# Idle TensorE products in front of each pair's inner-layer products and around each pair's sums in a graph-network kernel

## The chip, the cores and the metric

The kernel runs on one core of a Trainium2 chip. The metric is the device time of one execution, in microseconds. The kernel before takes 3646.17 us (median of 3 runs, 3644.92 to 3647.67 us).

## The reference: what is computed

Two graph layers over 6250 nodes of 128 channels and 200000 edges, sorted by target node:

```
h = relu(layernorm(x))
ef  = relu(edge_attr @ We1 + be1) @ We2 + be2          # 64 -> 128 -> 128 per edge
ef  = ef * sigmoid(edge_weight @ Wt + bt)
msg = relu(concat(h[src], ef) @ Wn1 + bn1) @ Wn2 + bn2
x = x + segment_sum(msg, dst) + h                      # first layer
h = relu(layernorm(x))
h = h + segment_sum(h[src], dst)                       # second layer
x = x + relu(relu(h @ W1 + b1) @ W2 + b2)
```

## The kernel before, in words

The edges are cut into 196 pairs of two blocks of 512 edges; four pairs make a body, so the first layer has 49 bodies. Four engines run streams of their own, tied by semaphores.

**First layer.** For each pair the engines take these steps.

- TensorE (`pair_step` in its stream): the inner-layer products of this pair (`hidden_products`, L787, f32, 512 columns, into `p_hid`), the message products of the pair two earlier (`message_products`, L804), the sums over the edges of the pair three earlier (`aggregate`, L815, and L818, whose end raises `agg_mm`), one window of edge counts for the second layer (`count_early`: L830, L836, L839; L836 multiplies one-hot tiles, 500 columns of 16-bit values, which VectorE makes just before), and the outer edge products of this pair (`edge_products`, L795, f32, 512 columns, whose end raises `ef_mm`). The next pair's L787 follows L795.
- VectorE: the one-hot tiles of the window (L1182, L1185), the message sums (L1134), the additions into `acc` (L1127, which wait for L818), two one-hot steps (L1140, L1147), the weighting (L1154, which waits for L795).
- ScalarE: relu of the inner layer (L630, waits for L787), sigmoid (L635), relu of messages (L640), counts out (L663, waits for L839).
- GpSimd: it issues the gathers of source rows, eight indirect transfers a pair (L537, in `gather_body`). Before the first four it waits for L795 of the pair before (`ef_mm`), before the last four for L818 (`agg_mm`).

**Second layer.** The edges of the hub nodes are covered by the counts; the rest are summed row by row in 64 pairs. For each pair TensorE's `sum_rows` waits for VectorE's one-hot tiles (`hot1_made`, L1085) and for the gathered rows, does 24 products of 64 columns (L915), and with the last frees the slot of the ring, which GpSimd's gather of a later pair waits for. Between the pairs stand windows of counts (`count_late`, again L836) and in three of eight pairs a chain of 98 products (`row_sums`, L925). Four pairs' rows are in the ring.

TensorE's stream is in order. PSUM bank 5 holds nothing during the second layer's sums.

Of the kernel before, what the change touches and what calls it, by code (L numbers as in the profile page):

```python
# [56 lines left out]
CK = CW * TP  # L57
# [25 lines left out]

NP3 = 3
NSLOT = 4


def gnn_program(nc, x, ea, ew, src, src_tiles, dst_tiles, dst_blocks, We1, be1, We2, be2, Wt, bt, Wn1, bn1, Wn2, bn2,
                W1, b1, W2, b2, out):
    ctx = ExitStack()  # L90
    with ctx:
        def sb(name, shape, dt=F32):
            return ctx.enter_context(nc.sbuf_tensor(name, shape, dt))

        def sem(name):
            return ctx.enter_context(nc.semaphore(name))
# [96 lines left out]
        iota_b = sb("iota_b", [P, P], F16)  # L193
        iota_k = sb("iota_k", [P, CK], F16)
# [9 lines left out]

        PARTS = NSLOT * GT * D * NP3 // 2
        parts = big[:, 0:PARTS].bitcast(BF16).rearrange("p (s t i d) -> p s t i d", s=NSLOT, t=GT, i=NP3)
        ef = sb("ef", [P, 2, BLK])
# [27 lines left out]
        BANK = 512  # L235
        ps = ctx.enter_context(nc.psum_tensor("ps", [P, 8 * BANK], F32))
        p_hid = [ps[:, q * BANK:(q + 1) * BANK] for q in (0, 1)]
# [5 lines left out]

        p_c = [ps[:, q * BANK:q * BANK + CK] for q in (0, 1)]
        p_c0 = ps[:, 2 * BANK:2 * BANK + CK]
        p_stored, p_own = (ps[:, q * BANK:q * BANK + CROW] for q in (2, 3))

        p_turn, p_prod = ([ps[:, q * BANK:q * BANK + GT * D].rearrange("p (t d) -> p t d", t=GT) for q in pair]
# [26 lines left out]
        table0_stored = sem("table0_stored")  # L275
        table1_stored = [sem(f"table1_stored{s}") for s in range(NSLOT)]

        ea_loaded = [sem(f"ea_loaded{u}") for u in range(RING)]
# [69 lines left out]
        def load_params(engine):  # L348

            return (engine.value_load(params[0:1, 0:1], min_val=1, max_val=MAX_SWEEPS),  # L350
                    engine.value_load(params[0:1, 1:2], min_val=0, max_val=NBODY - LBODY - 1),
                    engine.value_load(params[0:1, 2:3], min_val=LBODY + 1, max_val=MAX_SWEEPS * NBODY),
                    engine.value_load(params[0:1, 3:4], min_val=LBODY + 1, max_val=NBODY))
# [24 lines left out]
        def _(sp):  # L378
# [92 lines left out]
            for g in range(NG):  # L471
                sp.wait_ge(parts_made, g + 1)
                sp.dma_start(t1[:, g * GT:(g + 1) * GT, :], parts[:, g % NSLOT].rearrange("p t i d -> p t (i d)"))\
                  .then_inc(table1_stored[g % NSLOT], 16)

# [33 lines left out]
        def _(pool):  # L509
# [75 lines left out]
            for g in range(NG + 1):  # L585
# [3 lines left out]
                if g < NG:  # L589
                    pool.wait_ge(normed1, g + 1)  # L590
                    if g >= NSLOT:
                        pool.wait_ge(table1_stored[g % NSLOT], 16 * (g // NSLOT))
# [163 lines left out]
        def _(pe):  # L756
# [21 lines left out]
            pe.wait_ge(params_loaded, 16 * N_PARAMS)  # L778
            hot_f = hot[:, :, :, :, :].bitcast(F32)

            def hidden_products(b, u, n, first):
                pe.wait_ge(ea_loaded[u], b * 16 + 16)
                if not first:
                    pe.wait_ge(hid_made, n)
                for q in (0, 1):
                    k = slice(q * K_EDGE, (q + 1) * K_EDGE)
                    pe.matmul(p_hid[q], we1[k, :], ea_s[k, u, :], start=True, stop=True).then_inc(hid_mm, 1)  # L787
# [58 lines left out]
            def pair_step(b, u, since, window=None):  # L846
                n = b * (2 * RING) + 2 * u
                hidden_products(b, u, n, since == 0)
                if since >= 2:
                    message_products(n - 4, u % 2, since == 2)  # L850
                if since >= 3:
                    aggregate(n - 6, (u + 1) % 2, since == 3)
                if window:
                    count_early(*window)
                edge_products(n, since == 0)
# [24 lines left out]
            sweeps, start, total, bodies = load_params(pe)  # L880
# [26 lines left out]
            def sum_rows(b, u):  # L907

                n = b * (2 * RING) + 2 * u
                pe.wait_ge(hot1_made, n + 2)  # L910
                for q in (0, 1):
                    pe.wait_ge(gathered1[u][q], b * (16 * TB) + 16 * TB)
                    for t in range(TB):
                        for p in range(NP3):
                            i = pe.matmul(p_agg[:, q, 0, :], rows1[:, u, q, t, p, :], hot1[:, q, t, :],  # L915
                                          start=(t == 0 and p == 0), stop=(t == TB - 1 and p == NP3 - 1))
                i.then_inc(slot1_free, 1)

            def count_late(k, i):

                count_edges(k * CB + (NW0 + i), k * CB + (NW0 + i), p_c[i % 2], hot_src1, hot_key1, VT1, VH1)
# [18 lines left out]
            for u in range(RING):  # L940
                sum_rows(0, u)
                if u:
                    for i in range(4 * u - 4, 4 * u):
                        count_late(0, i)
                if u == RING - 1:
                    stored_rows(1, 2)
            with pe.Fori(1, NSTEP) as k:
                for t in range(2 * RING):
                    sum_rows(k * 2 + (t // RING - 1), t % RING)
                    if t == 0:  # L950
                        own_rows(k - 1, k * 3 - 2)
                    if t == 1:
                        stored_rows(k * 2, k * 3)
                    if t == 5:
                        stored_rows(k * 2 + 1, k * 3 + 2)
                    for i in SLOTS[t]:
                        count_late(k, i)
            own_rows(NSTEP - 1, 3 * NSTEP - 2)
            with pe.Fori(LBODY, total) as b:
                for u in range(RING):  # L960
                    sum_rows(b, u)
# [505 lines left out]
```

## Time and profile before

| | |
|---|---|
| median of 3 runs | 3646.17 us (3644.92 to 3647.67) |
| span of the profiled execution, first to last instruction | 3603.9 us |
| runs' median minus span | 42.3 us |
| TensorE busy | 2652.8 us (74%) |
| GpSimd busy | 2098.5 us (58%) |
| VectorE busy | 1962.6 us (54%) |
| ScalarE busy | 1009.1 us (28%) |
| mean granted TensorE clock | 0.804 of full |

The profile is of one execution; only its span is known of that execution, and its own time outside the span isn't. The difference of 42.3 us to the runs' median is taken as what lies around the span. The granted clock has two levels here, full (1.00, 2.4 GHz) and half (0.50, 1.2 GHz), so a mean of 0.804 says that the engine had half the clock for 39% of the span. "Idle before" names what ended an engine's idle time; "remote" is a release that the profile can't tie to one instruction.

### The profile page before, as it was taken

What the parts mean: (1) busy time and instruction counts of PE and PEld (TensorE: products, weight loads), DVE (VectorE), ACT (ScalarE), POOL (GpSimd) and SP (SyncE); (2) the same over time, 40 slices, a digit from 0 to 9 for tenths busy, and PEclk for the clock granted to TensorE, in tenths of its full rate; (3) what the DMA queues carried; (4) which work ended last, traced back from release to release, by engine and by line L of the source; (5) the groups of instructions that cost most, each with busy time, mean ns of one, the idle gap of its engine ahead of it and who ended that gap; (6) DMA issues with size and microseconds to landing.
All of it is one profiled execution on the core that took longest, in us unless ns stands there. A gap on an engine that the chain in (4) does not pass through costs nothing.

```text
span 3603.9 us, 51709 instructions
## 1 busy us (share of the span) xinstructions
PE 2652.8 (74%) x14584; PEld 1610.3 (45%) x14585; DVE 1962.6 (54%) x4063; ACT 1009.1 (28%) x1000; POOL 2098.5 (58%) x2125
## 2 busy tenths in 40 slices
PE   4687788877877778778877788785645766766766
PEld 3344444444444444444444444343332545544544
DVE  8665566655656566656655566665673333233333
ACT  3233333333333333333333333232231111111112
POOL 6566666666666666666666665555254555555552
PEclk8788888888888888878888888887875777877777
DMA  6444444444433343444344343333122434334332
GB/s 196 113 127 134 127 127 136 125 130 128 126 121 125 123 124 122 123 125 124 120 122 128 120 128 115 120 117 96 32 101 83 132 118 129 122 95 128 101 114 61
DMA packets 229418, 426.82 MB, mean 118 GB/s; under 512 B 82703, under 2 KB 141584, under 8 KB 229072
## 3 DMA queue, kind: packets, MB, share of 16 engines
q0 software_dynamic: 74752, 153.23, 16.3%
q1 hardware_dynamic: 103152, 177.42, 15.0%
q10 hardware_dynamic: 51266, 93.34, 7.4%
q8 instruction: 97, 1.59, 0.2%
q14 instruction: 151, 1.24, 0.1%
HBM read 364.35 MB, written 59.43 MB: 118 GB/s over the span
## 4 chain that ended last, share of the span: by engine, by line
PE 39%; issue 20%; DVE 17%; another core or an unknown queue 12%; DVEq 10%; SPq 1%; DMA 1%; ACT 0%; POOL 0%; ACTq 0%
PE ps L925 9%; PE ps L836 8%; PE ps L795 8%; DVE nodes L1185 5%; PE ps L804 5%; PE ps L815 4%; PE ps L787 3%; DVEq L1119 3%; DVEq L1165 2%; DVE hot L1140 2%; DVE acc L1127 1%; DVE arena L1185 1%; DVEq L1182 1%; PE ps L915 1%
## 5 line engine op out<-in xcount | busy, mean ns | idle before, releaser
L537 POOL DMA_INDIRECT big<-table,idx x2080 | 2032.9, 977 | 1375.8 <-issue 587.6
L836 PE MATMUL ps<-nodes 128*128 128x500 bf16 x1280 | 448.5, 469 | 335.8 <-DVE nodes L1185 180.3
L795 PE MATMUL ps<-arena,we 128*128 128x512 f32 x784 | 511.9, 784 | 29.7 <-issue 12.2
L640 ACT ACTIVATE big<-big 128x1024 f32<-128x1024 f32 x196 | 207.2, 1057 | 1074.3 <-DVE big L1134 917.5
L815 PE MATMUL ps<-hot,big 128*128 128x64 f32 x3136 | 395.9, 275 | 112.8 <-issue 86.0
L1185 DVE TENSOR_SCALAR nodes<-iota_k,win_off,nodes 128x500 bf16<-128x500 f16 x1280 | 453.7, 407 | 0.0
L815 PEld LDWEIGHTS ps<-hot,big 128*128 128x128 f32 x3136 | 381.6, 195 | 107.0 <-issue 104.6
L1182 DVE TENSOR_TENSOR nodes<-iota_b,nodes 128x384 bf16<-128x384 f16 (+1 forms) x492 | 245.4, 499 | 266.8 <-remote 174.8
L1134 DVE TENSOR_TENSOR big<-ps,big 128x1024 f32<-128x1024 f32 x196 | 239.3, 1221 | 244.2 <-issue 242.6
L836 PEld LDWEIGHTS ps<-nodes 128*128 128x128 bf16 x1280 | 106.3, 106 | 573.6 <-DVE nodes L1185 271.1
L630 ACT ACTIVATE arena<-ps,cols 128x1024 f32<-128x1024 f32 x196 | 218.5, 1115 | 418.7 <-PE ps L787 229.2
L719 ACT ACTIVATE arena<-ps 128x490 f32<-128x490 f32 x96 | 100.0, 1041 | 784.1 <-PE ps L839 601.4
L1127 DVE TENSOR_TENSOR acc<-ps,acc 128x128 f32 x392 | 113.9, 291 | 299.1 <-remote 250.3
L925 PE MATMUL ps<-acc,nodes 128*128 128x120 f32 x1568 | 225.1, 300 | 67.1 <-issue 60.6
L836 PE MATMUL ps<-arena 128*128 128x500 bf16 x384 | 167.5, 545 | 141.0 <-DVE arena L1185 114.4
L663 ACT ACTIVATE arena<-ps 128x490 f32<-128x490 f32 x192 | 199.1, 1037 | 236.8 <-remote 219.2
L1182 DVE TENSOR_TENSOR arena<-iota_b,arena 128x256 bf16<-128x256 f16 x192 | 80.9, 422 | 325.4 <-PE ps L836 178.9
L795 PEld LDWEIGHTS ps<-arena,we 128*128 128x128 f32 x784 | 172.9, 245 | 174.5 <-issue 169.4
L787 PE MATMUL ps<-arena,we 64*128 64x512 f32 x784 | 232.5, 669 | 22.7 <-DMA win_row<-win_d 18.2
L925 PEld LDWEIGHTS ps<-acc,nodes 128*128 128x128 f32 x1568 | 210.6, 215 | 77.6 <-issue 77.5
L635 ACT ACTIVATE arena<-arena,cols 128x1024 f32<-128x1024 f32 x196 | 240.9, 1229 | 0.0
L804 PEld LDWEIGHTS ps<-wn1b,ef 128*128 128x128 f32 x1568 | 187.2, 194 | 91.1 <-issue 91.1
(147 smaller groups left out, 2534.2 us busy)
## 6 DMA issues: line engine op xcount, KB each, us to landing
arena<-in_ew SPq DMA_DIRECT2D x196, 512.0 KB
arena<-in_ea SPq DMA_DIRECT2D x196, 256.0 KB
counts_d<-arena ACTq DMA_DIRECT2D x192, 245.0 KB
acc<-counts_d ACTq DMA_DIRECT2D x15, 2940.0 KB
big<-table,idx POOLq DMA_INDIRECT x2080
table<-big SPq DMA_DIRECT2D x7, 672.0 KB, 3.0
idx<-in_src SPq DMA_DIRECT2D x260, 4.0 KB
xs<-in_x SPq DMA_DIRECT2D x7, 448.0 KB, 5.5
```

Source lines behind the costliest of these rows:

```text
L537: pool.indirect_dma_start(to(u, q, t), None, table, bass.IndirectOffsetOnAxis(ap=idx[:, u, at:at + 1], axis=0))\
L630: act.activation(hid[:, :, :].rearrange("p q c -> p (q c)"), p_hid2, ACT.Relu, bias=be1_c).then_inc(hid_made, 2)
L635: act.activation(v, v, ACT.Sigmoid, bias=bt_c, scale=wt_c).then_inc(tw_made, 2)
L787: pe.matmul(p_hid[q], we1[k, :], ea_s[k, u, :], start=True, stop=True).then_inc(hid_mm, 1)
L795: pe.matmul(p_ef[q], we2[:, :], hid[:, q, :], start=True, stop=True).then_inc(ef_mm, 1)
L804: i = pe.matmul(p_pre[q][:, t * D:(t + 1) * D], efs[m][:, q, t * P:(t + 1) * P], wn1b[:, :], start=True, stop=True)
L815: pe.matmul(p_agg[:, q, 0, :], msg[:, m, q, t, :], hot_f[:, m, q, t, :], start=(t == 0), stop=(t == TB - 1))
L836: m = pe.matmul(to, hots[:, t, :], keys[:, t, :], start=False, stop=True, skip_group_check=True)
L925: m = pe.matmul(to, nodes[:, a, :], sums[:, :, a, :], start=(a == 0), stop=(a == NT - 1))
L1134: dve.tensor_tensor(msg[:, u % 2, :, :, :].rearrange("p q t d -> p (q t d)"), p_pre2, rows[:, u, :, :, :].rearrange("p q t d -> p (q t d)" ...
L1182: dve.tensor_tensor(hots[:, h * half:h * half + n, :], iota_v.to_broadcast([P, n, P]), half_src.to_broadcast([P, n, P]), ALU.is_equal)
L1185: m = dve.tensor_scalar(keys[:, h * half + t, :], iota_k[:, :], win_off[:, bass.ds(win, 1)], key[:, h * n + t:NTILE + VP][:, bass.ds(at, 1 ...
```

## The change

TensorE gets products whose results nobody reads: 128 x 128 constants times 128 x 500 constants, both 16-bit. Four stand in front of each pair's inner-layer products in the first layer (not before the first pair), and write to `p_hid[0]`, which the inner-layer products overwrite. In the second layer three stand in front of each pair's sums, ahead of all its waits, and three behind them; they write to bank 5. In `hidden_products` the wait for `hid_made` now stands ahead of the wait for the edge attributes.

```
+FILL0 = 4
+FILL1 = 3
...
+        p_idle = ps[:, 5 * BANK:5 * BANK + CK]
...
+            def idle_products(to, count):
+
+                for _ in range(count):
+                    pe.matmul(to, iota_b[:, :], iota_k[:, :], start=True, stop=True, skip_group_check=True)
+
             def hidden_products(b, u, n, first):
-                pe.wait_ge(ea_loaded[u], b * 16 + 16)
                 if not first:
                     pe.wait_ge(hid_made, n)
+                    idle_products(p_hid[0][:, 0:CK], FILL0)
+                pe.wait_ge(ea_loaded[u], b * 16 + 16)
...
             def sum_rows(b, u):
 
                 n = b * (2 * RING) + 2 * u
+                idle_products(p_idle, FILL1)
                 pe.wait_ge(hot1_made, n + 2)
...
                 i.then_inc(slot1_free, 1)
+                idle_products(p_idle, FILL1)
```

In TensorE's stream of the first layer, from one pair's window of counts to the next pair's, this stands before (`arena` is the edge data and the inner layer, `we` the edge weights, `big` the messages):

```order
L839 MATMUL ps<-zeros 128x2
L795 MATMUL ps<-arena,we 128x512 x2
L787 MATMUL ps<-arena,we 128x512 x2
L804 MATMUL ps<-wn1b,arena 128x128 x8
L815 MATMUL ps<-hot,big 128x64 x8
L818 MATMUL ps<-hot_sum,ones 1x2x64
```

and this in the changed kernel, whose line numbers are up to 13 higher:

```order
L850 MATMUL ps<-zeros 128x2
L806 MATMUL ps<-arena,we 128x512 x2
L789 MATMUL ps<-iota_k,iota_b 128x500 x4
L798 MATMUL ps<-arena,we 128x512 x2
L815 MATMUL ps<-wn1b,arena 128x128 x8
L826 MATMUL ps<-hot,big 128x64 x8
```

The four idle products stand between L795 (now L806) and L787 (now L798); all else keeps its order. A two-pair piece of TensorE's stream of the second layer, with two chains of row sums, before:

```order
L915 MATMUL ps<-hot,big 128x64 x24
L934 ISA
L935 ISA
L925 MATMUL ps<-arena,nodes 128x120 x49
L910 REGISTER_ALU
L915 MATMUL ps<-hot,big 128x64 x24
L929 ISA
L925 MATMUL ps<-acc,nodes 128x120 x49
```

and in the changed kernel:

```order
L789 MATMUL ps<-iota_k,iota_b 128x500 x3
L922 ISA
L924 ISA
L927 MATMUL ps<-hot,big 128x64 x24
L789 MATMUL ps<-iota_k,iota_b 128x500 x3
L947 ISA
L948 ISA
L938 MATMUL ps<-arena,nodes 128x120 x49
L789 MATMUL ps<-iota_k,iota_b 128x500 x3
L922 REGISTER_ALU
L927 MATMUL ps<-hot,big 128x64 x24
L789 MATMUL ps<-iota_k,iota_b 128x500 x3
```

Between a pair's sums (L915, now L927) and the next pair's there are now six idle products, on either side of the row sums (L925, now L938).

## Rows read from the trace of the kernel before

**Rows 1.** Windows, first and second layer: us, busy (x) of PE, PEld, DVE, ACT, POOL; clock, DMA.

```profile
200.00:2400.00 2200.00, 1742.63 (x8563) 986.83 (x8564) 1332.57 (x2566) 743.39 (x695) 1359.28 (x1391) 0.84 0.41 125
2725.00:3545.00 820.00, 562.32 (x4161) 393.80 (x4158) 271.69 (x837) 98.94 (x95) 459.63 (x480) 0.73 0.37 113
```

**Rows 2.** Groups of instructions: xcount, busy us, mean ns, idle before and its releasers.

```profile
L537 POOL DMA_INDIRECT big<-table,idx x2080 | 2032.9, 977 | 1375.8 <-issue 587.6 <-remote 408.6 <-PE ps L915 154.0
...
L787 PE MATMUL ps<-arena,we 64*128 64x512 f32 x784 | 232.5, 669 | 22.7 <-DMA win_row<-win_d 18.2 <-issue 3.2 <-DVE nodes L1052 1.3
...
L915 PE MATMUL ps<-hot,big 128*128 128x64 bf16 x1536 | 84.4, 224 | 54.2 <-DVE hot L1085 36.6 <-issue 17.2
```

**Rows 3.** Waits of GpSimd: us in total, times, longest us.

```profile
POOL big L537 <- remote: 408.6, 178, 3.7
POOL big L537 <- PE ps L915: 154.0, 25, 16.9
POOL big L537 <- PE ps L795: 125.0, 40, 8.8
```

**Rows 4.** Timeline of GpSimd, first layer, 1202 to 1254 us: start, busy, what, idle before.

```profile
1202.81 0.94 POOL L537 DMA_INDIRECT big<-table,idx  x1 [3.44 <-remote]
...
1211.36 0.94 POOL L537 DMA_INDIRECT big<-table,idx  x1 [3.69 <-PE ps L795]
...
1217.92 0.94 POOL L537 DMA_INDIRECT big<-table,idx  x1 [1.81 <-remote]
1230.09 0.94 POOL L537 DMA_INDIRECT big<-table,idx  x1 [2.06 <-remote]
1253.82 0.94 POOL L537 DMA_INDIRECT big<-table,idx  x1 [3.47 <-remote]
```

**Rows 5.** Timeline of TensorE, first layer, 1203 to 1225 us.

```profile
1203.94 2.86 PE L836 MATMUL ps<-nodes 128*128 128x500 bf16 x6 [7.36 <-DVE nodes L1185]
...
1206.85 3.61 PE L795 MATMUL ps<-arena,we 128*128 128x512 f32 x4
...
1215.04 0.25 PE L818 MATMUL ps<-hot_sum,ones 128*1 128x128 f32 x1
...
1215.33 1.45 PE L836 MATMUL ps<-nodes 128*128 128x500 bf16 x6
...
1216.81 1.98 PE L795 MATMUL ps<-arena,we 128*128 128x512 f32 x4
```

**Rows 6.** Windows around that place: us, busy of each engine, clock.

```profile
1199.90:1210.10 10.20, 6.16 (x11) 1.85 (x11) 6.21 (x13) 2.00 (x2) 3.94 (x4) 0.50 0.21 67
1210.20:1234.00 23.80, 21.67 (x135) 14.55 (x134) 16.18 (x31) 10.92 (x10) 14.81 (x16) 1.00 0.41 127
```

**Rows 7.** Timeline, first layer, one pair, 1172 to 1180 us.

```profile
1172.27 0.25 PE L818 MATMUL ps<-hot_sum,ones 128*1 128x128 f32 x1
...
1178.45 0.73 DVE L1127 TENSOR_TENSOR acc<-ps,acc 128x128 f32 x2 [5.32 <-remote]
...
1179.11 0.94 POOL L537 DMA_INDIRECT big<-table,idx  x1 [2.12 <-remote]
...
1179.88 1.97 PE L815 MATMUL ps<-hot,big 128*128 128x64 f32 x16 [1.10 <-DVE hot L1140]
```

**Rows 8.** Chain that ended last, 1200 to 1222 us: start, us, what.

```profile
1210.46 1.06 PE ps L787 x4
...
1218.79 1.06 PE ps L787 x4
```

**Rows 9.** Timeline of TensorE and GpSimd, second layer, 3351 to 3379 us.

```profile
3351.00 0.86 PE L915 MATMUL ps<-hot,big 128*128 128x64 bf16 x24
3351.70 8.53 PE L925 MATMUL ps<-acc,nodes 128*128 128x120 f32 x71
...
3352.68 0.94 POOL L537 DMA_INDIRECT big<-table,idx  x1 [11.60 <-PE ps L915]
...
3378.86 1.99 PE L836 MATMUL ps<-arena 128*128 128x500 bf16 x4 [1.94 <-issue]
```

## The prediction

> **What bounds the kernel now.** I read the windows of the two layers first, then the groups of instructions, then who waits for whom, and last the timelines of one body, engine by engine. The windows [rows 1] show TensorE as the busiest engine in both layers: 1743 of 2200 us in the first, 562 of 820 us in the second. A share of 79% is no bound by itself, though. It leaves 457 us idle in 2200 us.
>
> GpSimd's group [rows 2] shows the other pace. It has 2080 gathers of 0.977 us each with about 0.3 us of issue between, so 1.28 us a gather, 10.2 us for a pair's eight and 41 us for a body of four pairs. The timeline of GpSimd [rows 4] gives one body from 1202.81 to 1253.82 us, 51.0 us or 12.75 us a pair. The missing 10 us are the four waits that the reader sees in those rows, 3.44, 3.69, 1.81 and 2.06 us. Three of the four end by "remote". Over the kernel [rows 3] these are 178 waits of together 408.6 us, 2.3 us each on the mean, and only 40 waits (125.0 us) end by TensorE's L795 and 25 (154.0 us) by its L915. So the gathers set the pace for most pairs, and TensorE sets it at about 65 places.
>
> What the "remote" waits are is seen in one pair [rows 7]. L818 ends at 1172.27 + 0.25 = 1172.52 us, yet VectorE's addition, which waits for it, begins at 1178.45 and GpSimd's next gather, which waits for it too, at 1179.11 us. For some 6 us the ends of TensorE's products reach nobody, and they come when GpSimd's running gathers are through. I can't say what holds them. It matters here because work that TensorE does in such a stretch costs nothing.
>
> **The change part by part.** Nothing is removed. The wait for the edge attributes moves behind the idle products; L787 was idle 22.7 us in all its 784 instances, 18.2 us of it once for the window table, and no attribute transfer is among the releasers [rows 2]. The move costs nothing.
>
> *What is added.* 784 records of L787 are 196 pairs at four each, and the first pair gets none: 195 x 4 = 780 products. 1536 records of L915 are 64 pairs at 24 [rows 2]: 64 x 6 = 384 products. The price of one is that of L836, which has the same shape and also 16-bit operands: at full clock 1.45 us for six, so 0.24 us, and at half clock 2.86 us for six, 0.48 us [rows 5], or 1.99 us for four, 0.50 us [rows 9]. The mean clock of 0.84 in the first layer [rows 1] is 32% of the time at half, that of 0.73 in the second 54%. Mean price: first layer 0.68 x 0.24 + 0.32 x 0.48 = 0.32 us, four of them 1.27 us, 195 pairs 247 us. Second layer 0.46 x 0.24 + 0.54 x 0.49 = 0.38 us, six 2.25 us, 64 pairs 144 us. That is 391 us more work on TensorE, against 457 us idle in the first layer's window (2.65 us a pair) and 258 us in the second's (4.0 us a pair). It fits, if it falls where TensorE waits anyway.
>
> *First layer, where it falls.* The four stand between L795 and L787. In the chain of waits [rows 8] L787 stands twice in one body, at 1210.46 and at 1218.79 us, which would put eight products a body on the path. I follow the gathers instead. At 1210.46 us the clock has just become full (1.00 from 1210.2 on, 0.50 before [rows 6]), so four products cost 0.97 us. L818, at 1215.04 + 0.25 = 1215.29 us [rows 5], then ends at 1216.26 us. GpSimd goes on at 1217.92 us with four gathers begun at 1211.36 us ahead of that [rows 4], so 1.66 us are left and its handling of a release fits in. In the pair of [rows 7] the products and L787 and L804 behind them lie in the 6 us in which nobody sees TensorE's ends, and L815 waits 1.10 us for VectorE's one-hot tiles, which covers 0.97 us; without that cover it is 0.97 us a pair. What GpSimd waits for at 1211.36 us is L795, behind L836, and L836 began after 7.36 us of idle TensorE for VectorE's tiles [rows 5]: idle products earlier in the same step vanish in that gap. Bounds: none of the 40 waits on L795 lengthened, 0; all of them by four products at full clock, 39 us. Rows 5 and 7 both show the gap ahead, so I take an eighth, **+5 us**.
>
> *Second layer.* Here TensorE is itself late at 25 places [rows 3]. The row sums (L925) of one pair, 8.53 us and more in a row, stand between two L915, and GpSimd has sat idle for 11.60 us when the first of these L915 frees its slot [rows 9]. The three products behind an L915 run under the gathers that it lets go. The three ahead of the next L915 stand between the row sums and it, with no gap (L925 follows L915 at once, 3351.00 + 0.86 against 3351.70 us). So 25 x 3 x 0.24 = **+18 us**. Below: 0, if the late ends of L915 hide them all. Above: both sides at full clock, 25 x 6 x 0.24 = 36 us. At the other 39 pairs TensorE waits 0.5 to 2 us for VectorE ahead of L836 (1.94 us at 3378.86 [rows 9]) and the gathers set the pace.
>
> *The clock.* Idle products are work, and the clock follows work: while TensorE was busy 6.16 of 10.2 us with one 7.36 us gap before, it was at half; while busy 21.67 of 23.8 us, at full [rows 6, 5]. What would it give? In the body of [rows 5] L836 and L795 at half clock take 2.86 + 3.61 us where they take 1.45 + 1.98 us at full, 3.0 us more, and just these set free the gathers at 1211.36. But the idle products come behind L795, when the gap is over and the clock already rising. They don't fill the gap ahead of L836. In the first layer I take nothing back. In the second, the products behind L915 stand right in front of row sums that often begin at half clock; of 25 places I take 0.3 us each, about half of what three products at half clock cost more than at full (3 x 0.24 = 0.7), **-7 us**. Bounds: 0, and the first rival.
>
> The Trainium skill (TensorE: Matmul & The Clock Gate, Part 1) says that the throttled clock is the default and that activity releases it, and its section Why this matters advises keeping TensorE busy to hold the full clock. By that rule the change should be a gain of the first rival's kind. The trace agrees that the clock follows activity [rows 6]; whether these places are the right ones no row shows.
>
> *Sum.* Against the profiled span: 3603.9 + 5 + 18 - 7 = 3619.9 us. The median of the runs lies 42.3 us above the span: **3662 us**, 0.4% slower. Limits from the terms' bounds: 0 to +75 us without any clock effect, 3646 to 3721 us.
>
> **The rivals.**
>
> *The clock pays (faster).* For it: half clock for 32% and 54% of the two layers, and 3.0 us at one place of each body. Mechanism: the idle products lengthen busy stretches enough that the clock doesn't fall in the next short gap, and L836 and L795 then run at full clock and L795 lets the gathers go sooner. If one body in three gains the 3.0 us, 16 x 3.0 = 48 us; and of the second layer's 96 windows of counts a sixth at the path, 16 x (1.99 - 4 x 0.24) = 16 us. 3662 - 64 = 3598 us. It outweighs the cost from 16 us on, that is five bodies and nothing else. Against it: the long gaps, 7.36 us and more, lie ahead of L836, and nothing is put there.
>
> *All hidden (same).* The late ends and the gathers absorb everything: 3646 us.
>
> *The chain is right (much slower).* Four products twice in each of 48 bodies, 96 x 0.97 = 93 us, and both sides of the 25 late L915, 36 us: 3646 + 129 = 3775 us. For it: the chain [rows 8]. Against: it follows TensorE because TensorE is busy there, while the gathers' margin of 1.66 us lies beside it.
>
> **How the numbers follow.** A measurement of this kernel tells 0.2% (7 us) from no change. Forecast (3654 to 3715 us) 0.38, all hidden 0.22, the clock pays 0.30, the chain is right 0.10. Slower is 0.38 + 0.10 = 0.48, same 0.22, faster 0.30. The range, 3592 to 3705 us, leaves out the chain's case and the stronger half of the clock's, about 0.2. The slower side's own range is 3654 to 3715 us.
>
> **What the changed profile would show.** 1164 products of the new line, near 0.24 us each at full clock. Bodies of the first layer still near 51 us. GpSimd's waits for L795 (125 us) within 40 us of before, those for L915 up by 10 to 40 us. A mean granted clock a little above 0.80, mostly by the second layer. TensorE busy up by some 350 us. If the clock pays, the granted clock in the first layer is well above 0.84 and the waits for L795 fall. If the chain is right, bodies take 53 us. The prediction is wrong, above all, if the "remote" waits of 408.6 us shrink or grow, since I have no cause for them, or if the new products shift where the clock falls.

## The result and the profile after

The changed kernel took 3683.20 us (median of 4 runs, 3679.10 to 3698.16), the kernel before 3646.92 us beside it (4 runs, 3644.92 to 3652.77). The ratio is 1.0094, 95% interval 1.0067 to 1.0122: 34 us slower, between 24 and 44 us. The predicted 3662 us had the sign, and less than half of the size (+16 us).

The profiled execution of the changed kernel had an own time (its device time) of 3685.37 us and the span on the page's first line. TensorE's row says how busy it was:

```profile
span 3683.6 us, 53851 instructions
PE 2853.0 (77%) x15748; PEld 1711.8 (46%) x15749; DVE 1966.0 (53%) x4063; ACT 1010.1 (27%) x1000; POOL 2101.4 (57%) x2125
```

Only 1.8 us lie outside the span. So the 42.3 us that were put "around the span" of before are not there: the execution profiled before, of 3603.9 us, was itself some 40 us faster than the runs it stood beside. The experiments below show where such executions occur: on other chips the kernel before takes 3601, 3598 or even 2866 us. Which chip gave the first profile isn't on record. Spans of before and after are therefore not subtracted from each other here, and rows of the two are compared with care.

The windows of the two layers (the second lies 55 us later than in [rows 1], at the same place in the layer), columns as there:

```profile
200.00:2400.00 2200.00, 1829.59 (x9166) 1040.05 (x9165) 1312.85 (x2517) 736.34 (x688) 1339.00 (x1373) 0.87 0.40 123
2780.00:3600.00 820.00, 602.53 (x4322) 406.17 (x4323) 258.45 (x797) 95.84 (x92) 436.94 (x454) 0.80 0.35 107
```

The granted clock rose in both layers, from 0.84 to 0.87 and from 0.73 to 0.80 [rows 1], and yet GpSimd does no more in the same 2200 us (1339 us busy where it had 1359, 1.5% less; most of that can be the slower chip, as 3646.92 us are 1.2% more than the 3603.9 of the profile). TensorE's groups show what the clock did; columns as in [rows 2]:

```profile
L789 PE MATMUL ps<-iota_k,iota_b 128*128 128x500 f16 x1164 | 335.8, 407 | 32.8 <-DMA win_row<-win_d 20.8 <-issue 11.7
...
L927 PE MATMUL ps<-hot,big 128*128 128x64 bf16 x1536 | 67.2, 208 | 17.4 <-DVE hot L1098 17.3 <-issue 0.2
```

The 1164 new products (L789) took 335.8 us, but TensorE's busy time grew only from 2652.8 to 2853.0 us, by 200.2. Everything else on TensorE became 336 - 200 = 136 us shorter: the products kept the clock up and paid back 40% of themselves in TensorE's time. (Two executions on two chips of one speed, f0 and e0 below, give more: 332.9 us of products, busy time up by 146.8 us.) The sums of the pairs (L915, now L927) fell from 84.4 to 67.2 us, for instance. The kernel's time rose all the same, so what the clock gave back wasn't enough, or wasn't where the kernel's time is made. GpSimd's waits are nearer to that place; columns as in [rows 3]:

```profile
POOL big L542 <- remote: 374.2, 161, 3.4
POOL big L542 <- PE ps L927: 186.0, 25, 18.9
POOL big L542 <- PE ps L806: 143.0, 40, 13.5
POOL big L542 <- PE ps L829: 110.6, 46, 12.4
```

The waits for L927 grew from 154.0 to 186.0 us at the same 25 places, those for L806 from 125.0 to 143.0 us, at 40 places as before. New among the long ones is L829 (L818 before); "remote" fell by 34 us (from 408.6) at the same time.

**One late place in the second layer.** TensorE's timeline of the changed kernel:

```profile
2832.70 12.43 PE L938 MATMUL ps<-acc,nodes 128*128 128x120 f32 x98
2844.97 0.79 PE L789 MATMUL ps<-iota_k,iota_b 128*128 128x500 f16 x3
2845.60 0.86 PE L927 MATMUL ps<-hot,big 128*128 128x64 bf16 x24
2846.30 0.80 PE L789 MATMUL ps<-iota_k,iota_b 128*128 128x500 f16 x3
2846.93 8.42 PE L938 MATMUL ps<-arena,nodes 128*128 128x120 f32 x74
...
2862.04 1.08 PE L789 MATMUL ps<-iota_k,iota_b 128*128 128x500 f16 x3
2862.96 0.86 PE L927 MATMUL ps<-hot,big 128*128 128x64 bf16 x24
```

and GpSimd's beside it:

```profile
2847.35 0.94 POOL L542 DMA_INDIRECT big<-table,idx  x1 [18.88 <-PE ps L927]
...
2864.64 0.95 POOL L542 DMA_INDIRECT big<-table,idx  x1 [7.58 <-PE ps L927]
```

Each L927 frees a slot, and GpSimd, idle for 18.88 and 7.58 us, goes on 1.7 us after its beginning both times. Between the two L927 TensorE waits for no other engine. It only pauses inside the row sums, four times and 2.2 us in all, put down to `issue`. The three products behind the first push back the row sums (2846.30 to 2846.93, 0.63 us), the three ahead of the second push back L927 itself (2862.04 to 2862.96, 0.92 us). So both threes stand on the way from one late L927 to the next, 1.55 us together.

The same place can be found in every run on the chips near 3600 us. Without idle products (e0), and with only the three behind (f2, where the sums are L926), it is:

```profile
2800.90 0.86 PE L915 MATMUL ps<-hot,big 128*128 128x64 bf16 x24
...
2814.77 0.86 PE L915 MATMUL ps<-hot,big 128*128 128x64 bf16 x24
```

```profile
2787.51 0.86 PE L926 MATMUL ps<-hot,big 128*128 128x64 bf16 x24
...
2802.64 1.49 PE L926 MATMUL ps<-hot,big 128*128 128x64 bf16 x24
```

From start to start that is 13.87 us in e0 and 15.13 in f2. It is 13.93 us with six products of 2 columns (f3), 14.47 with the three ahead (f1), and 14.81 and 14.94 with all six (e2, f0). Part of the growth is `issue` pauses, 1.3 us in e0 and f3 and 1.5 to 1.8 us in the four others. With these taken off, the three behind still lengthen TensorE's way by 0.8 us, no less than the three ahead (0.3 us). The 17.36 us of the first measurement (2.2 us of pauses) are more than the products explain.

**The first layer** keeps its pace in the place that corresponds to [rows 4]. TensorE, and GpSimd under it:

```profile
1180.09 0.25 PE L829 MATMUL ps<-hot_sum,ones 128*1 128x128 f32 x1
...
1229.53 0.25 PE L829 MATMUL ps<-hot_sum,ones 128*1 128x128 f32 x1
```

```profile
1182.27 0.95 POOL L542 DMA_INDIRECT big<-table,idx  x1 [1.90 <-PE ps L829]
1194.57 0.94 POOL L542 DMA_INDIRECT big<-table,idx  x1 [2.56 <-remote]
1206.82 0.95 POOL L542 DMA_INDIRECT big<-table,idx  x1 [2.49 <-remote]
1225.04 0.94 POOL L542 DMA_INDIRECT big<-table,idx  x1 [2.87 <-PE ps L806]
1231.75 0.95 POOL L542 DMA_INDIRECT big<-table,idx  x1 [1.95 <-PE ps L829]
```

From 1182.27 to 1231.75 us it is 49.5 us for four pairs, no longer than the 51.0 of before. The waits have the lengths of the "remote" waits in [rows 4]; two of them now carry L829's name. They end 1.93 and 1.97 us after L829 does (1180.34 and 1229.78 us), so TensorE's end still reaches GpSimd late.

### The profile page after: what moved, and what is told of

Same layout as the page of the kernel before. It is cut to its first block, busy times and chain, and to the rows that moved or that the text cites. A ratio compares the mean times of both kernels' runs of the same rounds, so it can differ in the third digit from the quotient of the medians.

```text
span 3683.6 us, 53851 instructions
## 1 busy us (share of the span) xinstructions
PE 2853.0 (77%) x15748; PEld 1711.8 (46%) x15749; DVE 1966.0 (53%) x4063; ACT 1010.1 (27%) x1000; POOL 2101.4 (57%) x2125
## 4 chain that ended last, share of the span: by engine, by line
PE 43%; issue 22%; DVE 17%; DVEq 10%; another core or an unknown queue 8%; ACT 1%; DMA 1%; POOL 0%; ACTq 0%; SPq 0%
PE ps L938 9%; PE ps L847 8%; PE ps L806 6%; PE ps L815 5%; PE ps L826 5%; DVE nodes L1198 4%; PE ps L789 4%; PE ps L798 3%; DVEq L1178 2%; DVEq L1132 2%; DVE hot L1153 2%; DVE acc L1140 2%; DVE arena L1198 1%; DVEq L1195 1%
## 5 line engine op out<-in xcount | busy, mean ns | idle before, releaser
L847 PE MATMUL ps<-nodes 128*128 128x500 bf16 x1280 | 436.3, 464 | 262.4 <-DVE nodes L1198 161.3
L826 PE MATMUL ps<-hot,big 128*128 128x64 f32 x3136 | 411.2, 278 | 131.1 <-issue 125.3
L806 PE MATMUL ps<-arena,we 128*128 128x512 f32 x784 | 466.9, 723 | 19.3 <-issue 8.0
L826 PEld LDWEIGHTS ps<-hot,big 128*128 128x128 f32 x3136 | 394.4, 198 | 139.6 <-issue 137.5
L1147 DVE TENSOR_TENSOR big<-ps,big 128x1024 f32<-128x1024 f32 x196 | 239.5, 1222 | 314.1 <-issue 313.5
L789 PE MATMUL ps<-iota_k,iota_b 128*128 128x500 f16 x1164 | 335.8, 407 | 32.8 <-DMA win_row<-win_d 20.8
L938 PE MATMUL ps<-acc,nodes 128*128 128x120 f32 x1568 | 226.4, 301 | 71.0 <-issue 65.1
L847 PE MATMUL ps<-arena 128*128 128x500 bf16 x384 | 148.2, 486 | 140.2 <-DVE arena L1198 110.4
L938 PEld LDWEIGHTS ps<-acc,nodes 128*128 128x128 f32 x1568 | 215.1, 217 | 85.6 <-issue 83.9
L806 PEld LDWEIGHTS ps<-arena,we 128*128 128x128 f32 x784 | 160.2, 227 | 152.9 <-issue 147.7
```

Source lines behind the costliest of these rows:

```text
L789: pe.matmul(to, iota_b[:, :], iota_k[:, :], start=True, stop=True, skip_group_check=True)
L806: pe.matmul(p_ef[q], we2[:, :], hid[:, q, :], start=True, stop=True).then_inc(ef_mm, 1)
L826: pe.matmul(p_agg[:, q, 0, :], msg[:, m, q, t, :], hot_f[:, m, q, t, :], start=(t == 0), stop=(t == TB - 1))
L847: m = pe.matmul(to, hots[:, t, :], keys[:, t, :], start=False, stop=True, skip_group_check=True)
L938: m = pe.matmul(to, nodes[:, a, :], sums[:, :, a, :], start=(a == 0), stop=(a == NT - 1))
L1147: dve.tensor_tensor(msg[:, u % 2, :, :, :].rearrange("p q t d -> p (q t d)"), p_pre2, rows[:, u, :, :, :].rearrange("p q t d -> p (q t d)" ...
```

## Experiments

Each kernel was timed beside the kernel before on the same chip. The first four runs (e0 to e3) shared a chip on which that took 3601.35 us (35 runs, 3588.52 to 3628.26), the next four (f0 to f3) one with 3598.33 us (31 runs, 3588.76 to 3633.12). Single executions scatter by 15 us and more there, so verdicts rest on the ratios. "+17 us" is the ratio's distance from 1 in microseconds of that chip.

**e0: the kernel before once more, unchanged.** Its question is the 42.3 us.

> The kernel before, unchanged, profiled and timed again. The span profiled before the prediction was 3603.9 us, 42 us under the runs' median, while the changed kernel's profiled execution has a span of 3683.6 us and a time of 3685.4 us. Theory A: the first profile of the kernel before was of an unusually fast execution, and a second one has a span within 10 us of 3644 us. Theory B: the kernel before has 40 us outside its span, and its span is again near 3604 us.

Ratio 0.9994 (0.9974 to 1.0013). The profiled execution had an own time of 3599.99 us and a span of 3598.2. Both theories fell: nothing lies around the span, and the span isn't that of a fast execution among slower ones. This chip runs the kernel 1.2% faster than it ran at 3646.92 us in the first measurement, and the span of 3603.9 us is an ordinary one here.

**e1: idle products in the first layer only.**

```
-FILL1 = 3
+FILL1 = 0
```

> Idle products in the first layer alone (four a pair; none in the second). The whole change costs 36 us. Theory A (the cost is in both layers, in the first where GpSimd waits for L818): +15 to +25 us against the kernel before. Theory B (the prediction's sum: 5 us in the first layer): 0 to +8 us. Theory C (the clock pays in the first layer): below 0.

Ratio 0.9999 (0.9978 to 1.0020), between -8 and +7 us: theory B within the noise, 780 products for nothing. The clock in the window of the first layer was 0.87, e0's 0.83. GpSimd's waits in e0:

```profile
POOL big L537 <- remote: 402.8, 169, 3.7
POOL big L537 <- PE ps L915: 150.8, 25, 17.3
POOL big L537 <- PE ps L795: 128.4, 45, 8.0
...
POOL big L537 <- PE ps L818: 36.6, 10, 13.5
```

and in e1:

```profile
POOL big L542 <- remote: 328.6, 146, 3.4
POOL big L542 <- PE ps L806: 141.8, 39, 12.7
...
POOL big L542 <- PE ps L829: 130.5, 53, 13.9
```

The waits for L829 grow by 94 us and "remote" shrinks by 74; those for L806 grow by 13. Most of it is the same wait under another name, as the timeline above shows for the whole change. That a wait for a named instruction grew was no evidence of a cost.

**e2: idle products in the second layer only.**

```
-FILL0 = 4
+FILL0 = 0
```

> Idle products in the second layer alone (three ahead of and three behind each pair's sums). Theory A (cost in both layers): +12 to +22 us. Theory B (the prediction's sum, 11 us in the second layer): +5 to +15 us. If all of the cost is here: +30 us or more, and the first layer alone shows nothing.

Ratio 1.0048 (1.0023 to 1.0072): +17 us, between 8 and 26. The cost is in this layer; between the prices of theory A and theory B the run doesn't choose. GpSimd's waits for L927:

```profile
POOL big L542 <- PE ps L927: 190.9, 25, 15.7
```

They are 40 us above e0's 150.8 us, and the time grew by half of that. The growth isn't even: two of the 25 places have 19 us of it (12.74 us where e0 waits 3.35, and 13.11 where it waits 3.49). There TensorE does the row sums with pauses of up to 1.8 us put down to `issue`. Over the whole layer these pauses ahead of the row sums are 86.4 us in e2 and 65.8 in e0. In the other executions near 3600 us they lie between 63 and 78 us, and the waits for L927 mostly rise and fall with them. The pauses grew by half of what the waits grew by, and no run shows whether the products bring them on. The clock in the window of the second layer was 0.81, e0's 0.75.

**e3: both layers, products of 2 columns.**

```
-                    pe.matmul(to, iota_b[:, :], iota_k[:, :], start=True, stop=True, skip_group_check=True)
+                    pe.matmul(to[:, 0:2], iota_b[:, :], iota_k[:, 0:2], start=True, stop=True, skip_group_check=True)
```

> As many idle products at the same places, but of 2 columns in place of 500: the same number of instructions and weight loads, hardly any time on TensorE (L830, of 2 columns, starts 0.1 us ahead of the next product). Theory A (the cost is TensorE's time at places where it is late): within 8 us of the kernel before, and the granted clock as before. Theory B (the cost is by instruction, since ends of products reach others late when many are under way): most of the 36 us stays.

Ratio 1.0042 (1.0016 to 1.0069): +15 us, between 6 and 25. As many instructions, hardly any TensorE time in them, and it still costs. The middle is above theory A's 8 us and far below theory B's "most of the 36 us", so neither holds as it was put. Part of the cost seemed to go by the instruction, which f3 and g0 then followed up by layer.

**f0: the whole change again, on the second chip.**

> The whole change once more, beside the kernel before on this chip. Theory A (the costs of the two layers add up: 0 to 5 us from the first layer's products alone, 17 to 23 us from the second's): +15 to +28 us, with GpSimd's waits for L927 near 190 us and those for L829 near 110 us. Theory B (the two parts hurt each other, since the result read first was +36 us): +30 us or more. A span that lies within 2 us of the run's own time would show again that nothing of 40 us lies around the span.

Ratio 1.0072 (1.0038 to 1.0106): +26 us, between 14 and 38, theory A, though not with its waits near 190 us. It agrees with the first measurement (24 to 44 us) and with the sum of e1 and e2 (+17 us, each uncertain by some 8), so nothing demands that the two layers' products hurt each other. The own times of its runs went from 3599.11 to 3649.70 us. The profiled one was the fastest of the 8, its span 3597.3 us and GpSimd's waits for L927 158.1 us. In the first measurement these were 186.0 us, in e2 190.9. How much of the change shows depends on the execution, and one profile's waits for L927 are no measure of the cost.

**f1 and f2: second layer only, one side of the sums each.** f1 keeps the three ahead, f2 the three behind, both with `FILL0 = 0`. In f1:

```
                 i.then_inc(slot1_free, 1)
-                idle_products(p_idle, FILL1)
```

and, in f2, the three ahead go:

```
                 n = b * (2 * RING) + 2 * u
-                idle_products(p_idle, FILL1)
                 pe.wait_ge(hot1_made, n + 2)
```

> Second layer only, and there only the three products ahead of each pair's sums; none in the first layer. Theory A (what costs in the second layer is TensorE's time between the row sums and the next pair's sums, where TensorE is late): all of the 17 to 23 us stay, waits of GpSimd for L927 near 190 us. Theory B (each of the six products costs alike wherever it stands): half, +8 to +12 us, waits near 170 us. Theory C (the clock): less than 5 us.

> Second layer only, and there only the three products behind each pair's sums. Theory A (the time ahead of the next sums is what counts, and the products behind run under the gathers just let go): 0 to +5 us, waits for L927 near 150 us as without any. Theory B (each costs alike): +8 to +12 us, waits near 170 us.

Three ahead: ratio 1.0008 (0.9985 to 1.0030), +3 us, between -5 and +11. Three behind: 1.0020 (0.9995 to 1.0045), +7 us, between -2 and +16. That the three ahead carry the whole of e2's +17 us is outside f1's interval, though e2's low end of +8 us isn't. The side said to be free came out no cheaper. Halves of +8 us each lie inside both intervals, and so does 0. The waits for L927, 163.7 and 143.8 us, don't decide it either. f3's are 164.2 at no cost. What speaks against the free side is the one place above, 15.13 us with the three behind against 13.87 without.

**f3: second layer only, products of 2 columns on both sides.** e3's edit with `FILL0 = 0`.

> Second layer only, all six products a pair, but with 2 columns in place of 500, so that they take next to no TensorE time. Theory A (TensorE's time is the cost in the second layer): within 4 us of before, waits for L927 near 150 us, clock as before. Theory B (the cost comes with each instruction, whatever its length): +12 to +20 us, waits for L927 near 165 us or above.

Ratio 0.9997 (0.9976 to 1.0018), -1 us, between -9 and +6. In the second layer it is TensorE's time that costs, as theory A had it: 384 instructions without it cost nothing that can be measured. Only the waits for L927, 164.2 us, are where theory B had them. The interval lies below e2's, which begins at +8 us, though e2 ran on the other chip of this speed. It also makes e3's +15 us a cost of the first layer or of both together.

**g0: first layer only, products of 2 columns.** e3's edit with `FILL1 = 0`. This run and the next two shared a chip on which the kernel before took 2865.62 us (15 runs, 2859.19 to 2868.94), 20% less than on the two others.

> First layer only, four products a pair at the same place, with 2 columns in place of 500. Two columns in both layers had cost 15 to 20 us, and in the second layer alone 0 to 3 us. Theory A (in the first layer each idle product costs by its being there, not by its length, and with 500 columns a clock gain of the same size hides it): +10 to +18 us. Theory B (the first layer takes them for nothing, and the two-column run of both layers was high by chance): within 5 us of before.

Ratio 1.0015 (1.0006 to 1.0024): +4 us, between 2 and 7. By the letter theory B. But what the theories were to be told apart in is missing on this chip. GpSimd's waits, of which only `issue` (626.2 us) and one for the counts (23.2 us) are longer than these:

```profile
POOL big L598 <- ACT nodes L715: 18.9, 3, 17.0
POOL big L542 <- PE ps L829: 18.0, 19, 12.6
POOL big L542 <- PE ps L927: 10.3, 15, 1.6
```

There is no "remote" wait at all, where e3 has 153 of them with 338.3 us. The gathers themselves take as long as before (973 ns on the mean), but nothing stands between them. Its timeline of GpSimd around an L829:

```profile
810.01 0.94 POOL L542 DMA_INDIRECT big<-table,idx  x1 [0.31 <-issue]
811.25 0.94 POOL L542 DMA_INDIRECT big<-table,idx  x1 [0.30 <-PE ps L829]
```

and e3's, on the slower chip:

```profile
1109.66 0.94 POOL L542 DMA_INDIRECT big<-table,idx  x1 [3.48 <-PE ps L829]
```

**g1: first layer only, products in the gap.** The four stand ahead of the window of counts, where TensorE waits for VectorE's tiles, and write to the counts' bank ahead of its zeroing.

```
-                    idle_products(p_hid[0][:, 0:CK], FILL0)
...
                 pe.wait_ge(c_moved, moved)
+                idle_products(to, fill)
                 pe.matmul(to[:, 0:2], zeros[:, 0:P], zeros[:, 0:2], start=True, stop=False, skip_group_check=True)
```

`fill` is FILL0 in the first layer's windows and 0 in the second's.

> First layer only, with the four products of a pair moved from behind L806 to the window of counts, where TensorE waits for VectorE's one-hot tiles (they write to the counts' own bank, ahead of its zeroing). None in the second layer. Theory A (the prediction's: these gaps are where the clock falls, and the work there is free): a clock in the first layer above 0.87 and a time 10 to 40 us below before. Theory B (the gathers set the pace and a faster clock is worth nothing): within 7 us of before, whatever the clock. Theory C (the products push back L806, which stands behind them, where there is no gap): 7 us or more above before.

Ratio 1.0061 (1.0047 to 1.0074): +17 us, between 13 and 21: theory C by its number. Its reason isn't what the trace shows, for GpSimd's waits for L806 (L805 in g1) are 6.4 us where g0 has 5.5. The window 200 to 2400 us, of g0 and then of g1:

```profile
200.00:2400.00 2200.00, 1932.84 (x11444) 1196.77 (x11443) 1612.54 (x3197) 841.25 (x821) 1637.97 (x1672) 0.90 0.49 150
```

```profile
200.00:2400.00 2200.00, 1979.12 (x11362) 1185.71 (x11361) 1611.65 (x3181) 844.98 (x822) 1623.29 (x1658) 0.95 0.49 148
```

The clock in this window is the highest of all runs, 0.95, and the kernel is slower. The trace shows where the time stays. Near the end of the layer stands a window with many visits, which VectorE paces. g0's TensorE enters it at 2021.98 us:

```profile
2021.98 1.45 PE L847 MATMUL ps<-nodes 128*128 128x500 bf16 x6
```

g1's at 2041.46 us, right behind its idle products:

```profile
2040.41 1.02 PE L789 MATMUL ps<-iota_k,iota_b 128*128 128x500 f16 x4
2041.46 1.45 PE L847 MATMUL ps<-nodes 128*128 128x500 bf16 x6
```

GpSimd begins to wait at 2052.2 us (2076.33 - 24.16), 3.9 us later than in g0, where the same wait ended at 2055.49 us after 7.18 us:

```profile
2076.33 0.95 POOL L542 DMA_INDIRECT big<-table,idx  x1 [24.16 <-DVE big L1147]
```

TensorE had fallen 19.5 us behind g0's and had held up the gathers by no more than 3.9. Here GpSimd needs a pair done that stands behind the long window, and the wait ends 20.8 us later than in g0. The whole loss was paid at one place.

**g2 and h0: second layer only, and nothing beside row sums.** Of eight pairs, five keep the three ahead and five the three behind. The last eight pairs, behind the loop, have both.

The new arguments of `sum_rows` say whether the products ahead and those behind are there:

```
-                    sum_rows(k * 2 + (t // RING - 1), t % RING)
+                    sum_rows(k * 2 + (t // RING - 1), t % RING, t not in (1, 2, 6), t not in (0, 1, 5))
```

> Second layer only, three ahead and three behind as in the change, but left out on the sides at which row sums (L938) stand: of eight pairs, five keep the three ahead and five the three behind. Theory A (only next to the row sums is TensorE late, there both sides stand on its own chain to the next L927 and count alike, and elsewhere the gathers hide them): within 5 us of before, waits of GpSimd for L927 near 150 us. Theory B (each product costs alike wherever it stands): five eighths of 17 to 23 us, +11 to +14 us. A gain of over 7 us would say that the clock in the second layer is worth something once the late places are spared.

> The kernel with no idle products beside the row sums and none in the first layer once more. It had run on a chip where the kernel before takes 2866 us and GpSimd's waits on remote releases are absent, and gained 0.44% there. If this chip is of the kind at 3600 us: theory A (the cost is where row sums stand beside the products, on TensorE's own chain) expects within 7 us of before or a gain up to 13 us, and waits for L927 near 150 us; theory B (each product costs alike) expects +11 to +14 us and waits near 175 us. If it is of the kind at 2866 us: again 10 to 16 us below before.

g2: ratio 0.9956 (0.9942 to 0.9970), -13 us, between -17 and -9. h0, the same kernel on such a chip again (before 2863.19 us, 11 runs): 0.9967 (0.9955 to 0.9979), -9 us, between -13 and -6. This version beats the kernel before there. Theory B's +11 to +14 us are out for this kind of chip. Theory A isn't tested by it, since the late L927 that it speaks of are missing here (6.1 us of waits). The second layer's window is denser and faster. First g0, whose second layer has no idle products, then g2:

```profile
2150.00:2780.00 630.00, 506.85 (x4102) 364.77 (x4102) 277.73 (x810) 93.83 (x90) 468.05 (x484) 0.76 0.49 152
```

```profile
2150.00:2780.00 630.00, 528.37 (x4484) 379.57 (x4485) 282.04 (x828) 95.94 (x92) 475.42 (x490) 0.89 0.50 152
```

The clock goes from 0.76 to 0.89 and GpSimd gets 490 gathers and other instructions in, where it had 484. The layer's first gather is 2.4 us earlier than in g0, its last (2810.61 and 2819.85 us) 9.2 us earlier, and the last sums begin 17.8 us earlier. So about half of the difference is made behind the last gather. The last sums of rows in g0, waiting for VectorE:

```profile
2830.30 1.46 PE L927 MATMUL ps<-hot,big 128*128 128x64 bf16 x24 [1.54 <-DVE hot L1098]
2833.30 1.46 PE L927 MATMUL ps<-hot,big 128*128 128x64 bf16 x24 [1.54 <-DVE hot L1098]
```

and in g2:

```profile
2808.92 1.43 PE L789 MATMUL ps<-iota_k,iota_b 128*128 128x500 f16 x6
2810.63 0.87 PE L927 MATMUL ps<-hot,big 128*128 128x64 bf16 x24 [0.28 <-DVE hot L1098]
```

The idle products fill the wait for L1098, and the sums take 0.87 us in place of 1.46. This is a gain of the kind that the first rival expected, though in the other layer: TensorE waits anyway, and behind the last gather only TensorE and VectorE are left to finish. Neither run says what g2 does on the slower kind of chip, nor what the whole change does on this one. So it stays open how much of the gain is the place and how much the chip.

## Why the prediction was right, and where it was off

**The sign and the place.** The cost is in the second layer (e2 +17 us, between 8 and 26; e1 between -8 and +7), and there in TensorE's time (f3). Both were forecast. That it arises at the 25 pairs whose L915 GpSimd waits for fits the traces, but no run shows it on such a chip. "The chain is right" (+129 us) and "all hidden" are out. That 3683 us lie in the range of 3592 to 3705 says little, since the range also holds no change and a clear gain; the forecast of "slower" had a chance of 0.48.

**The sum's first error: the 42.3 us.** The step "the median of the runs lies 42.3 us above the span" took a difference between two measurements for something around each execution. The profiled executions show 1.8 us there. The step was harmless by luck: the 3662 us came out beside 3646 because the same 42.3 us were added that the faster execution had taken away. It left the +16 us alone, so the chance of being slower didn't hang on it. But the prediction took durations from a faster execution than the runs it was held against.

**First layer, +5 us.** Measured 0 (between -8 and +7), consistent. The eighth that was taken for the 40 waits on L795 is too small a term for any run to test. TensorE's ends still reach GpSimd 1.9 us after they occur, with the idle products in front. What was not foreseen is e3 against f3: +15 us with 2 columns in both layers and -1 us in the second alone leave some 16 us (uncertain by 12) to the first. 500 columns cost nothing there. The reading that fits is a price by the instruction which the better clock pays back, but g0, meant to show it, ran on a chip without the late ends and found +4 us. It is argued, not shown.

**Second layer, +18 us.** The step that failed is "the three products behind an L915 run under the gathers that it lets go". They do, and they still push back the row sums and with them the next L915, which is the late one. At the one place followed above the way from L915 to L915 grows from 13.87 to 15.13 us with the three behind alone, to 14.47 with the three ahead alone, and to 14.81 and 14.94 with all six. The timed runs f1 and f2 can't tell the sides apart. So the term should have counted six products, 36 us before the clock gives anything back. GpSimd's waits for L927 are a poor measure of it: they grew by 32 us in the first measurement and by 40 in e2, but stand at 158.1 us in f0, and in e2 `issue` pauses grew by half as much beside them. By the 1 us or so of that place, 25 places make some 25 us, an estimate. The timed costs are +17 (e2), +26 (f0) and +34 us. That only TensorE's time matters was right (f3). One reading behind the term was wrong: the 1.94 us ahead of L836 in [rows 9] end by `issue`, not by VectorE, as the sum had it for the other 39 pairs.

**The clock, -7 us.** "A mean granted clock a little above 0.80, mostly by the second layer": it was 0.841, with +0.07 in the second layer and +0.03 in the first, where nothing had been expected. "TensorE busy up by some 350 us": 200.2, since other products became 136 us shorter. The size of the clock's effect was underrated, and the worth of it wasn't: in e1 the first layer's clock was 0.87 for e0's 0.83, and nothing was gained. The likely reason, that what waits for TensorE there gets its ends late or waits for the gathers, is argued and not tested. What the clock gave back in the second layer no run isolates.

**The sign of being wrong.** "Above all, if the 'remote' waits of 408.6 us shrink or grow": they shrank, to 374.2 us, and in e1 from 402.8 to 328.6 us at an unchanged time. The waits were mostly renamed. The sign was a bad one, since it moves without the time.

The Trainium skill (TensorE: Matmul & The Clock Gate, Part 1) has it that the default state is throttled and activity releases it. The windows above agree: with 500-column products the clock went from 0.84 to 0.87, 0.73 to 0.80, 0.90 to 0.95 and 0.76 to 0.89. Its section Why this matters advises keeping TensorE busy. By the runs that alone is worth nothing: over the whole execution g1 and g2 had the same clock (0.915 and 0.917), and g1 lost 17 us while g2 gained 13.

**What stays open.** The first measurement's +34 us is more than e1 and e2 add up to, though the intervals meet. The kernel before was slower by 1.2% there, and no part was run on that chip alone. Whether the `issue` pauses inside the row sums grow because of the products is open too, and so is what g2's placement is worth where the ends come late.

## What to carry to other kernels

Work put into an engine's stream is free only where that engine waits before the next thing that somebody else awaits; follow it to that next end, since work "behind" a signal is still ahead of the following one. In these runs a higher clock paid only where the engine's end was waited for, so read the waits of the consumer and not the granted clock. And when a wait changes the name of its releaser, compare the time of the stretch before calling it a new cost. A profile is of one execution: where executions scatter as much as the effect, follow one place through several runs.

## What the runs showed of the hardware

**The same program took 3647, 3601, 3598, 2866 and 2863 us in five sessions.** The last four were on four different chips; the first chip isn't on record. On the two fastest, GpSimd's "remote" waits (402.8 us, 169 of them in e0) are absent, and so is TensorE's idle time put down to `issue`. L826, the sums over the edges, in e3:

```profile
L826 PE MATMUL ps<-hot,big 128*128 128x64 f32 x3136 | 414.2, 277 | 223.7 <-issue 209.8 <-DVE hot L1153 12.9
```

and in g0:

```profile
L826 PE MATMUL ps<-hot,big 128*128 128x64 f32 x3136 | 374.3, 273 | 1.6 <-DVE hot L1153 1.6
```

Both take 273 to 277 ns a product; the 210 us between them are gone. The kinds of chip differ by some 730 us, twenty times the change studied. All waits of GpSimd other than `issue` are 860 us in e0 and 103 us in g0, so the difference is one of waiting and not of slower work. How much of it comes from TensorE's ends being seen late, and why the chips differ, no run here shows.
